# A scan's weight loading and constant building moved into the stage before it

## The chip, the cores and the metric

The kernel runs on one core of a Trainium2 chip. The metric is the device time of one execution in microseconds (us); the time given for a kernel is the median of its runs. The engines are named as in the profile: PE (TensorE, matrix products), PEld (its weight loads), DVE (VectorE), ACT (ScalarE), POOL (GpSimd) and SP (SyncE, which here only issues transfers). Each engine runs its own program in order, and semaphores tie the programs together.

## The reference, cut to what matters

Four sublayers follow one another, each with a residual and a layer norm: a scan, a mixture of experts, an attention and a second mixture of experts. The change lies in the first. Its reference:

```python
x_sub = x[:, ::2]                                      # 2048 of 4096 tokens, 256 features
x_sub = x_sub * rsqrt(mean(square(x_sub), -1) + EPS) * g_norm
xz = einsum('bld,ed->ble', x_sub, w_in) + b_in         # 512 wide
x_proj, gate = split(xz, 2, axis=-1)
c_sum = Cm.sum(axis=0)                                 # Cm is [256, 64]
def step(h, xt):                                       # h is [B, 256, 64]
    h = tanh(h * A + xt[:, :, None] * Bm)
    y = h @ c_sum + Dv * xt
    return h, y
h_last, ys = scan(step, h0, swapaxes(x_proj, 0, 1))
out = swapaxes(ys, 0, 1) * silu(gate)
out = repeat(einsum('bld,ed->ble', out, w_out) + b_out, 2, axis=1)
```

## The kernel before

The scan sublayer runs in stages: `project_in`, `load_scan_weights`, `scan_chunks`, and then `project_out`. Each stage is a block in which every engine has a program of its own. At the end of a block all engines meet, so that nothing of the next stage starts before the slowest engine of the last one has come.

`project_in` works on the 2048 tokens in four chunks of 512 (NC = 4, CH = 512); the 256 features lie on 128 partitions in DH = 2 halves. SP issues the loads of the tokens (L86), of `g_norm`, `b_in` and `w_in` (L89 to L93), and eight stores of zeros, 1 MB each, into the DRAM tensor `inbox` (L97), which a later stage needs. DVE squares the tokens (L121), PE sums the squares over the features with a matrix of ones, into PSUM bank c for chunk c (L144), ACT takes the root (L170), DVE the reciprocal (L125), and DVE scales the tokens (L128, two halves each). PE then makes four products for each chunk (L159): e = 0 and 1 are x_proj, which ACT copies into `xpT` (L176, semaphore `drained`), and e = 2 and 3 are the gate, of which ACT takes the sigmoid (L181) and DVE makes silu (L135, semaphore `gated`). PE may write a bank again only when it is drained or gated. In DVE's program all eight instructions of L135 come after all four chunks of L125 and L128. POOL has nothing in this stage but five memsets and the identity matrix (L102 to L108).

`load_scan_weights` has five transfers on SP: A, Bm, Cm and Dv (L194, L195) and a store of `xpT` to the DRAM tensor `x_proj` (L197, semaphore `x_saved`). When the four loads have landed, DVE copies A into PSUM (L209) and PE sums Cm over the features with the ones matrix into bank 1 (L203); DVE copies that sum twice into `csum` (L211, L212).

`scan_chunks` cuts the sequence into eight chunks that are scanned side by side, each with a warm-up of WARM = 20 steps: (20 + 256) = 276 steps in all, in blocks of BL = 12. In every step, in three groups, DVE multiplies the state by A (L280) and adds x times B (L285), and ACT takes tanh (L360). POOL makes the products x times B ahead of DVE (L334), with room for RING_X = 4 steps; its x comes from a slab that ACT copies (L349). PE makes the outputs of a block of 12 steps after that block is done, with 64 diagonal matrices, one for each state, as its weights (L379). DVE builds these ahead of its first step: it clears the first state (L262) and then writes 64 matrices of 128x128, each the identity times one column of `csum` (L264). They lie in the tile `stream`, which is free until the scan is over. `x_saved` is waited for by DVE before it overwrites `xpT`, after the third block.

## Time and profile before

| | |
|---|---|
| median of 3 runs | 3964.82 us (3960.57 to 3975.85) |
| the profiled execution's own time | 3958.41 us |
| its span, first to last instruction | 3956.8 us |
| mean granted clock of PE, as a share of full speed | 0.906 |
| `project_in` (to the end of the last L135) | 0 to 53.89 us |
| `load_scan_weights` (to the end of L212) | 53.89 to 59.39 us |
| `scan_chunks` before its first step (first L280) | 59.39 to 79.64 us |
| the scan's steps, to the last output | 79.64 to 808.9 us |

A row of the time line gives the start in us, the length in us, engine, line, operation, the tile written and the tiles read, shapes, the number of instructions merged into the row, and in square brackets how long the engine was idle before and what ended that. Merged rows are as long as from the first start to the last end.

### The profile page before, as it was taken

The page shows a single profiled execution, that of the slowest core. Times are in us where ns is not written, and L with a number is a line of the kernel's source. Part 1 is how long each engine was busy: PE and PEld are TensorE (multiplying, and loading weights), DVE is VectorE, ACT ScalarE, POOL GpSimd, SP SyncE. Part 2 cuts the span into 40 slices and gives each one's busy share as a digit, 9 for nine tenths or more (in the row PEclk, how much of TensorE's full clock was granted, in tenths as well). Part 3 has the DMA queues.
Part 4 walks back from the last instruction along what each step waited for, and adds up shares of the span by engine and source line. Part 5 has one row for each costly group of instructions (what it writes and reads, how often), then busy time and mean ns, then how long its engine had stood idle before and what let it go on. Part 6 is the DMA issues. An engine that isn't in the chain of part 4 may idle for free. (4 is left out here: it accounts for less than half of the span.)

```text
span 3956.8 us, 70342 instructions
## 1 busy us (share of the span) xinstructions
PE 3296.1 (83%) x25130; PEld 2356.1 (60%) x25130; DVE 2956.1 (75%) x5189; ACT 1989.2 (50%) x4068; POOL 1121.4 (28%) x1381
## 2 busy tenths in 40 slices
PE   4477776780799956799999999999999955999997
PEld 1477776740688855544555555555555424888886
DVE  7999999941344446688888888888889406888888
ACT  2544444410444412256777777777777832333333
POOL 2888888705222242000111111112021030000000
PEclk7788888875899967788999999999999977999999
DMA  3000000012222135520303031221200000000001
GB/s 135 1 1 0 0 0 0 0 46 105 94 85 85 53 100 158 119 38 7 45 13 45 13 45 24 36 35 26 42 18 11 9 24 9 13 12 12 12 12 43
DMA packets 85212, 150.95 MB, mean 38 GB/s; under 512 B 16625, under 2 KB 53382, under 8 KB 83251
## 3 DMA queue, kind: packets, MB, share of 16 engines
q1 hardware_dynamic: 64626, 104.12, 10.9%
q0 software_dynamic: 19584, 42.14, 3.5%
q10 hardware_dynamic: 768, 1.57, 0.3%
q8 instruction: 146, 2.39, 0.3%
q14 instruction: 88, 0.71, 0.1%
HBM read 90.60 MB, written 57.41 MB: 37 GB/s over the span
## 5 line engine op out<-in xcount | busy, mean ns | idle before, releaser
L1724 DVE TENSOR_REDUCE row_max<-psum 128x2 f32<-128x1024 f32 (+2 forms) x1152 | 1250.4, 1131 | 219.1 <-PE psum L1598 164.2
L1677 ACT ACTIVATE probs_T<-psum 128x512 f32<-128x512 f32 (+3 forms) x2304 | 1120.8, 566 | 366.0 <-PE psum L1622 283.6
L1622 PE MATMUL psum<-q_rows,k_rows 50*128 50x512 f32 (+3 forms) x2304 | 771.6, 440 | 15.1 <-ACT probs_T L1677 11.5
L379 PE MATMUL psum<-h_hist,stream 128*128 128x192 f32 x2816 | 502.8, 344 | 246.4 <-ACT h_hist L360 246.4
L1598 PE MATMUL psum<-k_rows,q_rows 48*128 48x512 f32 (+3 forms) x2304 | 641.1, 451 | 39.3 <-DVE row_max L1724 23.8
L334 POOL TENSOR_TENSOR x_times_b<-x_slab,B_sb 128x384 f32<-128x384 f32 (+1 forms) x828 | 625.4, 818 | 149.3 <-DVE psum L285 91.1
L379 PEld LDWEIGHTS psum<-h_hist,stream 128*128 128x128 f32 x2816 | 496.4, 203 | 252.7 <-ACT h_hist L360 154.6
L1642 PE MATMUL psum<-probs_T,v_all 128*17 128x256 f32 (+1 forms) x8704 | 600.3, 378 | 1.0 <-issue 1.0
L1622 PEld LDWEIGHTS psum<-q_rows,k_rows 50*128 50x128 f32 x2304 | 364.7, 187 | 328.5 <-ACT probs_T L1677 278.3
L360 ACT ACTIVATE h_hist<-psum 128x384 f32<-128x384 f32 (+1 forms) x828 | 339.4, 453 | 378.4 <-DVE psum L285 378.4
L1972 PE MATMUL psum<-x_T,w_part 128*128 128x512 f32 x1632 | 404.3, 397 | 24.8 <-POOL w_part L2032 24.8
L1598 PEld LDWEIGHTS psum<-k_rows,q_rows 48*128 48x128 f32 x2304 | 286.9, 191 | 151.7 <-DVE row_max L1724 96.3
L285 DVE TENSOR_TENSOR psum<-psum,x_times_b 128x384 f32<-128x384 f32 (+1 forms) x828 | 372.9, 508 | 0.0
L280 DVE TENSOR_TENSOR psum<-h_hist,psum 128x384 f32<-128x384 f32 (+1 forms) x828 | 371.2, 506 | 0.5 <-ACT h_hist L360 0.2
L1642 PEld LDWEIGHTS psum<-probs_T,v_all 128*17 128x17 f32 x8704 | 210.5, 97 | 259.4 <-ACT probs_T L1677 80.9
L1972 PEld LDWEIGHTS psum<-x_T,w_part 128*128 128x128 f32 x1632 | 301.0, 190 | 85.5 <-POOL w_part L2032 24.9
L1567 POOL DMA_DIRECT2D o_raw<-o_acc x64 | 37.0, 578 | 1092.1 <-ACT o_acc L1689 1057.6
L2071 DVE SCALAR_TENSOR_TENSOR stream<-psum,comb,stream 128x256 f32<-128x256 f32 x544 | 236.4, 476 | 0.6 <-PE psum L1984 0.6
L1984 PEld LDWEIGHTS psum<-w_part,hidden_T 128*128 128x128 f32 x1632 | 214.4, 192 | 28.6 <-DVE hidden_T L2057 15.6
L1984 PE MATMUL psum<-w_part,hidden_T 128*128 128x256 f32 x1632 | 219.4, 285 | 14.2 <-DVE hidden_T L2057 14.2
L832 PE MATMUL psum<-xeT_part,w_part 128*128 128x512 f32 x768 | 183.2, 398 | 25.4 <-ACT hT_part L873 12.8
L2032 POOL TENSOR_TENSOR w_part<-attn_T,w_part 128x768 fp32r<-128x768 f32 x17 | 31.5, 1853 | 599.1 <-ACT w_part L1996 493.7
(212 smaller groups left out, 3260.2 us busy)
## 6 DMA issues: line engine op xcount, KB each, us to landing
w_raw<-in_w SPq DMA_DIRECT2D x16, 1024.0 KB, 8.4
qk_rows<-qk_split SPq DMA_DIRECT2D x64, 256.0 KB, 3.0
q_rows<-qk_rows SPq DMA_DIRECT2D x42, 256.0 KB, 12.0
k_rows<-qk_rows SPq DMA_DIRECT2D x42, 256.0 KB, 16.8
inbox<-zeros SPq DMA_DIRECT2D x8, 1024.0 KB, 10.5
xe_sb<-inbox SPq DMA_DIRECT2D x8, 1024.0 KB, 6.0
outbox<-ye_sb POOLq DMA_DIRECT2D x8, 1024.0 KB, 10.4
o_raw<-o_acc POOLq DMA_DIRECT2D x64, 128.0 KB, 2.1
```

The costliest lines, as they stand in the source:

```text
L280: dve.tensor_tensor(part(ha, i), part(prev, i), over_chunks(A, i), ALU.mult).then_inc(ha_ready, 1)
L285: dve.tensor_tensor(u(i), part(ha, i), part(xb[:, t % RING_X], i), ALU.add).then_inc(u_ready, 1)
L334: pool.tensor_tensor(out, x, b, ALU.mult).then_inc(xb_ready, 1)
L360: act.activation(part(hist[:, slot, t], i), u(i), ACT.Tanh).then_inc(h_ready, 1)
L379: last = pe.matmul(ps[:, 1 + j, 0:BL * DH * CHUNKS], diag[:, s, :], hist[:, j, :, :, :].rearrange("p t h (s c) -> p (t h) s c", s=NS)[:, : ...
L1598: last = pe.matmul(ps[:, bank_of_S(s, j), 0:width], q[at, b, i * P:(i + 1) * P], kk[at, b, mm * CH:mm * CH + width], start=True, stop=not ...
L1622: last = pe.matmul(ps[:, bank, o:CH], kk[at, b, kt * P:(kt + 1) * P], q[at, b, qc * CH + o:(qc + 1) * CH], start=True, stop=not diag)
L1642: last = pe.matmul(ps[at:at + HD + 1, 7, lo:HALF], k.v[:, kt, 2 * (n // 4) + j, :], pt[:, u % RING_P, j, HALF * half + lo:HALF * (half + 1 ...
L1677: act.activation(pt[:, u % RING_P, j, o:CH], ps[:, S_BANKS + at_item % RING_ST, o:CH], ACT.Exp, scale=SCALE).then_inc(taken, 1)
L1724: dve.tensor_reduce(mx[:, n % 4, heads[0]:heads[-1] + 1, QT * c + i % QT, mm], ps[:, banks, 0:width], AX.X, ALU.max).then_inc(maxed, 1)
L1972: last = pe.matmul(ps[:, 2 * half + c % 2, :], w_part[:, b, wp, at:at + INTER], xT[:, xp, h, c * CH:(c + 1) * CH], start=(n == 0 and h == ...
L1984: last = pe.matmul(ps[:, 4 + 2 * (c % 2) + s // 2, (s % 2) * D:(s % 2 + 1) * D], hT[:, c % 2, hp, s * P:(s + 1) * P], w_part[:, b, wp, WCO ...
```

## The change

Nothing of the computation changes. The stage `load_scan_weights` is gone. Its four loads stand in `project_in` on SP, behind the token loads and ahead of the `inbox` stores; the store of `x_proj` stands behind these, after a wait for all eight drained halves. PE sums Cm between its first and its second chunk of products, after a wait for the four loads and for ACT's last root (bank 1 holds chunk 1's sums until then). DVE copies the sum and A between its last scaling and its first gate. POOL builds the diagonal matrices, 16 at a time, four instructions, when the first copy of the sum is there; PE's wait for them in the scan is now for `k.diags` at 4.

```diff
@@ project_in
+        cm = sb("cm_sb", [P, DH, NS])
+        diag = k.stream[:, :, :].rearrange("p n c -> p (n c)").rearrange("p (s q) -> p s q", s=NS)
...
         @block.sync
...
+            for dst, src in ((k.A, a["A"]), (k.B, a["Bm"]), (cm, a["Cm"])):
+                sp.dma_start(dst[:, :, :], src.rearrange("(h p) s -> p h s", p=P)).then_inc(ab_in, 16)
+            sp.dma_start(k.Dv[:, :], a["Dv"].rearrange("(h p) -> p h", p=P), allow_slow_non_contiguous=True).then_inc(ab_in, 16)
             sp.wait_ge(k.zeros_ready, 1)
...
+            sp.wait_ge(drained, DH * NC)
+            sp.dma_start(a["x_proj"].rearrange("(h p) t -> p h t", p=P), k.xpT[:, :, WARM:WARM + TP]).then_inc(k.x_saved, 16)
+            sp.wait_ge(ab_in, 64)
...
         @block.gpsimd
...
+            pool.wait_ge(const_ready, 5)
+            pool.wait_ge(copied, 1)
+            for s in range(0, NS, 16):
+                pool.tensor_tensor(diag[:, s:s + 16, :], k.ident[:, :].unsqueeze(1).to_broadcast([P, 16, P]),
+                                   k.csum[:, 0, s:s + 16].unsqueeze(2).to_broadcast([P, 16, P]), ALU.mult).then_inc(k.diags, 1)
...
         @block.vector
...
+                if c == NC - 1:
+                    dve.wait_ge(csum, 1)
+                    dve.tensor_copy(k.csum[:, 0, :], ps[:, 1, 0:NS]).then_inc(copied, 1)
+                    dve.tensor_copy(k.csum[:, 1, :], ps[:, 1, 0:NS]).then_inc(copied, 1)
+                    dve.tensor_copy(ps[:, 0, 0:DH * NS].rearrange("p (h s) -> p h s", h=DH), k.A[:, :, :]).then_inc(a_copied, 1)
...
         @block.tensor
...
+                if c == 1:
+                    pe.wait_ge(ab_in, 64)
+                    pe.wait_ge(root, NC)
+                    for h in range(DH):
+                        last = pe.matmul(ps[:, 1, 0:NS], k.ones[:, :], cm[:, h, :], start=(h == 0), stop=(h == DH - 1))
+                    last.then_inc(csum, 1)
...
-def load_scan_weights(nc, k, a):
...
@@ scan_chunks
-            for s in range(NS):
-                last = dve.tensor_scalar(diag[:, s, :], k.ident[:, :], k.csum[:, 0, s:s + 1], None, ALU.mult)
-            last.then_inc(diags, 1)
...
-            pe.wait_ge(diags, 1)
+            pe.wait_ge(k.diags, 4)
...
@@ build_scan
-        load_scan_weights(nc, k, a)
```

DVE's program from its last scaling in `project_in` to its first steps in the scan, before (a row is a line of the kernel, the operation, the tiles and the shape; branches end a stage's program):

```order
L128 SCALAR_TENSOR_TENSOR xsT<-xsT,g_norm_sb,rms 128x512 x2
L135 SCALAR_TENSOR_TENSOR gateT<-psum,b_in_sb,gate_sig 128x512 x8
L64 UNCONDITIONAL_BRANCH
L206 UNCONDITIONAL_BRANCH
L209 COPY psum<-A_sb 128x128
L211 COPY csum_sb<-psum 128x64
L212 COPY csum_sb<-psum 128x64
L186 UNCONDITIONAL_BRANCH
L260 UNCONDITIONAL_BRANCH
L262 MEMSET h_hist 128x1024
L264 TENSOR_SCALAR stream<-ident,csum_sb 128x128 x64
L280 TENSOR_TENSOR psum<-h_hist,psum 128x384 x2
```

The same stretch of DVE's program now:

```order
L142 SCALAR_TENSOR_TENSOR xsT<-xsT,g_norm_sb,rms 128x512 x2
L146 COPY csum_sb<-psum 128x64
L147 COPY csum_sb<-psum 128x64
L148 COPY psum<-A_sb 128x128
L154 SCALAR_TENSOR_TENSOR gateT<-psum,b_in_sb,gate_sig 128x512 x8
L64 UNCONDITIONAL_BRANCH
L254 UNCONDITIONAL_BRANCH
L256 MEMSET h_hist 128x1024
L271 TENSOR_TENSOR psum<-h_hist,psum 128x384 x2
```

The three copies moved from between the stages to ahead of the gates, and the 64 instructions that build the matrices left DVE.

POOL's program from the end of its constants to its first products of the scan, before:

```order
L106 MEMSET zeros 128x256
L108 ISA
L108 AFFINE_SELECT ident<-ident 128x128
L64 UNCONDITIONAL_BRANCH
L320 UNCONDITIONAL_BRANCH
L334 ISA
L334 TENSOR_TENSOR x_times_b<-x_slab,B_sb 128x8x48 x2
L334 TENSOR_TENSOR x_times_b<-x_slab,B_sb 128x2x8x16
```

The same stretch of POOL's program now:

```order
L115 MEMSET zeros 128x256
L117 ISA
L117 AFFINE_SELECT ident<-ident 128x128
L122 TENSOR_TENSOR stream<-ident,csum_sb 128x2048 x4
L64 UNCONDITIONAL_BRANCH
L311 UNCONDITIONAL_BRANCH
L325 TENSOR_TENSOR x_times_b<-x_slab,B_sb 128x8x48 x2
L325 TENSOR_TENSOR x_times_b<-x_slab,B_sb 128x2x8x16
```

Four instructions of 2048 elements on each partition stand now between the identity matrix and the end of POOL's stage.

SP's program, all of it up to the end of the scan's set-up, before:

```order
L86 DMA xsT<-in_xs_T 128x2x512 x3
L97 DMA inbox<-zeros 128x8x256 x8
L64 UNCONDITIONAL_BRANCH
L191 UNCONDITIONAL_BRANCH
L194 DMA A_sb<-in_A 128x2x64
L194 DMA B_sb<-in_Bm 128x2x64
L194 DMA cm_sb<-in_Cm 128x2x64
L195 DMA Dv_sb<-in_Dv 128x2x1
L197 DMA x_proj<-xpT 128x2x2048
```

The same stretch of SP's program now:

```order
L89 DMA xsT<-in_xs_T 128x2x512 x3
L99 DMA A_sb<-in_A 128x2x64
L99 DMA B_sb<-in_Bm 128x2x64
L99 DMA cm_sb<-in_Cm 128x2x64
L100 DMA Dv_sb<-in_Dv 128x2x1
L103 DMA inbox<-zeros 128x8x256 x8
L106 DMA x_proj<-xpT 128x2x2048
```

The four loads moved ahead of the eight stores of zeros, and the store of `x_proj` follows these within the same stage.

## Rows read from the trace of the kernel before

**Rows 1.** Busy us of each engine (instructions), PE's clock, DMA share, by stretch:

```profile
35.00:54.00 19.00, 17.38 (x40) 7.46 (x40) 5.04 (x7) 6.87 (x10) 0.00 (x0) 1.00 0.00 0
60.00:80.00 20.00, 0.00 (x0) 0.00 (x0) 20.00 (x66) 0.05 (x1) 9.52 (x12) 0.50 0.10 44
```

**Rows 2.** Time line of DVE, 30 to 83 us:

```profile
32.81 1.41 DVE L128 SCALAR_TENSOR_TENSOR xsT<-xsT,g_norm_sb,rms 128x512 f32<-128x512 f32 x2
34.15 1.40 DVE L135 SCALAR_TENSOR_TENSOR gateT<-psum,b_in_sb,gate_sig 128x512 f32<-128x512 f32 x2
...
53.14 0.75 DVE L135 SCALAR_TENSOR_TENSOR gateT<-psum,b_in_sb,gate_sig 128x512 f32<-128x512 f32 x1 [0.97 <-ACT gate_sig L181]
57.86 0.29 DVE L209 COPY psum<-A_sb 128x128 f32<-128x128 f32 x1 [3.98 <-DMA Dv_sb<-in_Dv]
59.04 0.22 DVE L211 COPY csum_sb<-psum 128x64 f32<-128x64 f32 x1 [0.88 <-PE psum L203]
...
59.96 0.91 DVE L262 MEMSET h_hist<- 128x1024 f32 x1 [0.56 <-PEq L186]
60.79 18.93 DVE L264 TENSOR_SCALAR stream<-ident,csum_sb 128x128 f32<-128x128 f32 x64
79.64 1.34 DVE L280 TENSOR_TENSOR psum<-h_hist,psum 128x384 f32<-128x384 f32 x3
...
82.17 1.00 DVE L280 TENSOR_TENSOR psum<-h_hist,psum 128x384 f32<-128x384 f32 x2
```

**Rows 3.** Time line of PE, several stretches from 19 to 810 us:

```profile
20.24 12.23 PE L159 MATMUL psum<-xsT,w_in_sb 128*128 128x512 f32 x24 [2.76 <-DVE xsT L128]
...
34.95 17.43 PE L159 MATMUL psum<-xsT,w_in_sb 128*128 128x512 f32 x40 [2.47 <-DVE gateT L135]
57.88 1.12 PE L203 MATMUL psum<-cm_sb,ones 128*128 128x64 f32 x4 [5.50 <-DMA Dv_sb<-in_Dv]
...
141.47 23.82 PE L379 MATMUL psum<-h_hist,stream 128*128 128x192 f32 x128 [82.47 <-ACT h_hist L360]
...
785.70 22.59 PE L379 MATMUL psum<-h_hist,stream 128*128 128x192 f32 x128 [8.12 <-ACT h_hist L360]
```

**Rows 4.** Time line of ACT, 24 to 60 us:

```profile
29.08 0.69 ACT L181 ACTIVATE gate_sig<-psum,b_in_sb 128x512 f32<-128x512 f32 x1 [0.34 <-PE psum L159]
...
52.42 0.69 ACT L181 ACTIVATE gate_sig<-psum,b_in_sb 128x512 f32<-128x512 f32 x1 [1.03 <-PE psum L159]
59.69 0.36 ACT L349 ACTIVATE x_slab<-xpT 128x192 f32<-128x192 f32 x1 [6.59 <-PEq L186]
```

**Rows 5.** Time line of SP, the issues of transfers, 0 to 1000 us:

```profile
3.02 1.49 SPq L86 DMA_DIRECT2D xsT<-in_xs_T  x3
4.55 23.03 SPq L97 DMA_DIRECT2D inbox<-zeros  x8
...
56.12 0.47 SPq L197 DMA_DIRECT2D x_proj<-xpT  x1
```

**Rows 6.** Transfers, 0 to 200 us: issues, KB each, median us to landing:

```profile
inbox<-zeros SPq DMA_DIRECT2D x8, 1024.0 KB, 10.5
...
Dv_sb<-in_Dv SPq DMA_DIRECT2D x1, 1.0 KB, 2.2
```

**Rows 7.** POOL's groups by shape, whole span (busy us, mean ns, idle before):

```profile
L938 POOL TENSOR_TENSOR w_part<-w_raw,w_part 128x2048 fp32r<-128x2048 f32 x8 | 36.8, 4602 | 94.7 <-ACT w_part L859 94.7
...
L2032 POOL TENSOR_TENSOR w_part<-attn_T,w_part 128x768 fp32r<-128x768 f32 x17 | 31.5, 1853 | 599.1 <-ACT w_part L1996 493.7 <-ACT w_part L2012 105.4
```

**Rows 8.** Time line of POOL, 0 to 90 us (idle in brackets):

```profile
60.14 9.52 POOL L334 TENSOR_TENSOR x_times_b<-x_slab,B_sb 128x384 f32<-128x384 f32 x12 [58.21 <-ACT x_slab L349]
...
84.05 2.26 POOL L334 TENSOR_TENSOR x_times_b<-x_slab,B_sb 128x384 f32<-128x384 f32 x3 [0.26 <-DVE psum L285]
```

**Rows 9.** L264 alone, by stretch: busy us of DVE (instructions begun), clock, DMA:

```profile
64.00:66.00 2.00, 2.00 (x3) 0.50 0.00 0
72.00:76.00 4.00, 4.00 (x22) 0.50 0.00 0
```

More of the change, by code:

```diff
@@ L78, in project_in @@
             "inv_rms_ready", "xz_ready", "xz_drained", "gate_sigmoid", "gate_done"))
+        cm = sb("cm_sb", [P, DH, NS])
+        ab_in, csum, copied, a_copied = (sem(n) for n in ("ab_in", "csum_ready", "csum_copied", "a_copied"))
+        diag = k.stream[:, :, :].rearrange("p n c -> p (n c)").rearrange("p (s q) -> p s q", s=NS)
         NC = TP // CH
@@ L181, in _ @@
                         act.activation(sig[:, n % 2, :], ps[:, 4 + n % 2, :], ACT.Sigmoid, bias=b[:, e:e + 1]).then_inc(sigmoid, 1)
-def load_scan_weights(nc, k, a):
-    with ExitStack() as loc:
-        cm = k.sbuf(loc)("cm_sb", [P, DH, NS])
-        ab_in, csum, copied, a_copied = k.sem("ab_in"), k.sem("csum_ready"), k.sem("csum_copied"), k.sem("a_copied")
-        block = loc.enter_context(nc.Block())
-        @block.sync
-        def _(sp):
-            for dst, src in ((k.A, a["A"]), (k.B, a["Bm"]), (cm, a["Cm"])):
-                sp.dma_start(dst[:, :, :], src.rearrange("(h p) s -> p h s", p=P)).then_inc(ab_in, 16)
-            sp.dma_start(k.Dv[:, :], a["Dv"].rearrange("(h p) -> p h", p=P), allow_slow_non_contiguous=True).then_inc(ab_in, 16)
-            sp.dma_start(a["x_proj"].rearrange("(h p) t -> p h t", p=P), k.xpT[:, :, WARM:WARM + TP]).then_inc(k.x_saved, 16)
-        @block.tensor
-        def _(pe):
-            pe.wait_ge(ab_in, 64)
-            for h in range(DH):
-                last = pe.matmul(k.psum[:, 1, 0:NS], k.ones[:, :], cm[:, h, :], start=(h == 0), stop=(h == DH - 1))
-            last.then_inc(csum, 1)
-        @block.vector
-        def _(dve):
-            dve.wait_ge(ab_in, 64)
-            dve.tensor_copy(k.psum[:, 0, 0:DH * NS].rearrange("p (h s) -> p h s", h=DH), k.A[:, :, :]).then_inc(a_copied, 1)
-            dve.wait_ge(csum, 1)
-            dve.tensor_copy(k.csum[:, 0, :], k.psum[:, 1, 0:NS]).then_inc(copied, 1)
-            dve.tensor_copy(k.csum[:, 1, :], k.psum[:, 1, 0:NS]).then_inc(copied, 1)
 def scan_chunks(nc, k, a):
@@ L237, in scan_chunks @@
         count = sb("seam_count", [P, 1])
-        xs_ready, xb_ready, ha_ready, u_ready, h_ready, y_done, y_taken, h_zero, diags, warm_kept = (
-            sem("ch_" + n) for n in ("xs", "xb", "ha", "u", "h", "y_done", "y_taken", "h_zero", "diag", "warm"))
+        xs_ready, xb_ready, ha_ready, u_ready, h_ready, y_done, y_taken, h_zero, warm_kept = (
+            sem("ch_" + n) for n in ("xs", "xb", "ha", "u", "h", "y_done", "y_taken", "h_zero", "warm"))
         compared, counted, summed, told = (sem("ch_" + n) for n in ("compared", "counted", "summed", "told"))
@@ L2109, in build_program @@
         k.x_saved = k.sem("x_saved")
+        k.diags = k.sem("diags")
         k.zeros_ready, k.inbox_zeroed = k.sem("zeros_ready"), k.sem("inbox_zeroed")
```

## The prediction

> **What bounds the kernel now.** I read the page's slices first, to see that the change touches only the first stages. Then come the busy times by stretch: while the input projection runs, from 35 to 54 us, PE is busy for 17.38 of 19 us and POOL for none; from 60 to 80 us DVE is busy all the time and PE for none [rows 1]. So between the projection and the scan DVE alone sets the pace, and ahead of it POOL has nothing to do.
>
> DVE's time line gives that stretch step by step [rows 2]. The last gate ends at 53.14 + 0.75 = 53.89 us. The copy of A then waits 3.98 us for the last of the four loads, the copy of the sum for PE, and the stage ends at 59.39. The memset of the scan begins 0.57 later and takes 0.91. The 64 diagonal matrices take from 60.79 to the first step at 79.64. From the last gate to the first step 25.75 us pass, in which no step of the scan runs. All the stages are bound by meetings of the engines, so a microsecond taken out here is one off the whole, as long as what follows keeps its length.
>
> **What the diagonal matrices are needed for.** PE's first output in the scan starts at 141.47 us, 62 us after the first step, and waits for ACT's states [rows 3]. The matrices are early by far; they cost time only since they stand ahead of the steps in DVE's program.
>
> **The change part by part.**
>
> 1. The loads. A, Bm, Cm and Dv are issued behind the last token load, so from about 4.5 us on [rows 5]. Alone Dv landed 2.2 us after its issue; the slowest kind here, the stores of zeros, took 10.5 [rows 6]. A load issued by 6.5 us that takes as long as those lands at 17 us. PE asks for it after its first chunk, which ends at 29.0 us: the second gate sigmoid of that chunk waits for PE until 29.08 [rows 4]. Cost: none. The wait for the last root is over too: in ACT's program all four roots stand ahead of these sigmoids. What this removes is the wait for the loads in the old stage. The stores of zeros move back by four issues, some 2 us; SP ends their issue at 27.58 [rows 5] and has nothing then until 50 us, so nothing waits.
>
> 2. The sum of Cm on PE took 1.12 us at low clock [rows 3]. It now delays the second chunk's first two products by at most that. These end at 20.24 + 12.23 = 32.47, and PE then idles for 2.47 us until the first gate is done [rows 3]. The cover is larger than the cost; without it the cost would be 1.12 us.
>
> 3. The three copies on DVE stand now between the last scaling (end 34.22) and the first gate [rows 2]. The gate frees the bank that PE waits for, so they do cost: twice 0.22 and 0.29, 0.73 us by their lengths, and 0.29 if the shorter ones are hidden by overlap [rows 2]. I take 0.73. From that gate on the rest of the projection is one chain: PE's 17.43 us without a gap [rows 3], ACT's last sigmoid at 52.42 [rows 4], the last gate [rows 2]. So the last gate ends at 53.89 + 0.73 = 54.62.
>
> 4. The matrices on POOL. 4 x 2048 = 8192 elements on each partition. A two-input POOL instruction of 2048 elements took 4602 ns [rows 7]: 4 x 4.602 = 18.4 us. The nearest rows on either side: 2.26 us for the 1024 elements of one step, with broadcast operands as here, gives 18.1 [rows 8]; 1853 ns for 768 gives 19.8, and the first twelve products, 9.52 us for 4096, give 19.0 [rows 7, 8]. POOL can start when the first copy of the sum is there, 34.22 + 0.22 = 34.44, so it ends at 52.9 (52.5 to 54.2). That is ahead of the last gate at 54.62: hidden, by 1.7 us at my value and 0.4 at the slow end. Every microsecond beyond would be paid in full at the meeting.
>
> 5. Into the scan. One stage and one meeting are gone. From the end of a stage's last DVE instruction to the memset 0.57 us, then 0.91, and the first step may start: 54.62 + 1.48 = 56.1 us, against 79.64. POOL's head start in x times B is gone too: before it had 12 products ready, now it starts just ahead of DVE. ACT's slab starts 0.30 after the stage's end and takes 0.36 [rows 4], POOL 0.09 later, at 55.4; it makes a step's products in 2.26 us [rows 8], so by 57.6. DVE's adds of the first step begin when its three multiplications are through, at 56.1 + 1.34 = 57.4 [rows 2]. The first add needs only the first product, by 56.2 (9.52/12 = 0.79 us each) [rows 8], and the third product is there by 57.6, when DVE has still two adds ahead of it. A step of DVE takes 2.53 us (79.64 to 82.17) [rows 2], and POOL, faster by 0.26, draws ahead. Cost: none.
>
> 6. The store of `x_proj` is issued when the last half is drained, some 6 us ahead of 56.12 [rows 5]. It is needed after the third block, 36 steps on. No cost.
>
> 7. The scan's end. After the last step DVE waits for PE's last block of outputs, 22.59 us in this execution; the first block took 23.82 [rows 3]. Which of the two falls to the last block depends on how PE's clock stands at that moment, and a shifted start may change it: 0 to 1.2 us, taken as 0, since the scan's own pattern is unchanged.
>
> Sum: 79.64 - 56.1 = **23.5 us saved**. By the bounds: 24.0 with overlapped copies; 19.5 if, against every row, POOL ended 4 us after the gates. Against the profiled execution's own time: 3958.41 - 23.5 = 3934.9. That execution lies 6.4 us under the median of the runs shown, so for the median I say 3964.82 - 23.5 = 3941.3, rounded to **3941**.
>
> **A rule weighed against the rows.** Beside POOL's first products DVE began 3 of its matrices in 2 us, alone 22 in 4 us [rows 9]: 0.67 against 0.18 us each. The two engines do block one another here. The Trainium skill, SBUF — State Buffer, section Who interferes with whom, says that they share one pair of ports as an exclusive lock, that `tensor_scalar` can take it, and that a DVE instruction with at most one SBUF input outside the two-port modes does not contend. By that rule the gates (one input from PSUM, one from SBUF) would not be held up by POOL. The scan's adds, with the same kinds of input, keep their step of 2.53 us beside POOL [rows 2, 8], so the trace agrees.
>
> The rows above put POOL's instruction at 4602 ns; for the same matrices DVE took 18.9 us [rows 2]. The Trainium skill, GPSIMD Engine Reference, section When to use GPSIMD, advises against elementwise work there, as about twice as slow as DVE. Taken against DVE's 18.9 us that would be 38 us of POOL. The rows don't bear it out for this case, since DVE's time was 64 short instructions, half of them beside POOL; but it is a rival.
>
> **The rivals.**
>
> A. POOL's build is late. What speaks for it is the small margin, 1.7 us, and a shape that no row shows (2048 elements, both operands broadcast). Each us beyond 54.62 counts. At twice DVE's 18.93, 37.9 us, POOL ends at 72.3 and 17.7 of the 23.5 are given back: 3959. At 3 ns an element, 24.6 us, it ends at 59.0: 3946. All four POOL rows lie between 2.2 and 2.4 ns an element. Chance 0.08.
>
> B. The four loads are caught among the 8 MB of zeros. The zeros are issued until 27.58, by then 2 us later, and take 10.5 more [rows 5, 6]: 40 us at the worst. PE's second chunk would start 11 us late, of which its 2.5 us of idle time cover some: about 8 us lost, 3949. Against it: they are issued ahead of all the zeros. Chance 0.05.
>
> C. The scan's pace falls, the slower side. Without its head start, POOL must keep DVE's pace from the first step. The point from which it decides is a product time of 2.53 us a step; from 2.53 + 23.5/276 = 2.62 us on the kernel is slower than before. At 2.70 us a step it loses 0.17 x 276 = 47 us and gains 23.5: 3988. For it: the beginning ran at 9.52/4 = 2.38 a step, not 2.26. Against it: in all the later steps POOL waits 0.26 us for DVE, so the pace is shown over the whole scan [rows 8]. Chance 0.03.
>
> D. The change doesn't bring what it says: the start of the scan moves forward, but the time is lost again behind it (PE's clock in the last outputs, or the stages after). Then the time stays between 3950 and 3965. Nothing in the rows names more than 1.2 us. Chance 0.04.
>
> **How the numbers follow.** The forecast has 0.80, A 0.08, B 0.05, C 0.03, D 0.04. About 0.5%, or 19.8 us, is what a measurement can tell from no change here, so faster begins at 3945.0. The three runs before spread over 15 us, and a median of runs may well be 4 us off; 3941 lies 4 under the bound. I give the forecast 0.85 to be told as faster: 0.68, and 0.02 from the milder half of A. The rest of the forecast (0.12), most of A, B and D are within 0.5%: 0.27. C is slower, 0.03. The range for 8 in 10: downwards the profiled execution's own basis, 3935, less 3 us; upwards the spread of the runs, A at 3 ns and B, 3951.
>
> **What would show it.** The first multiplication of a step at 56 us (55.5 to 58), the last gate at 54.6, POOL's four instructions at 4.5 to 4.8 us each with the last end ahead of that gate, PE without a wait for the loads between its first two chunks, steps of 2.52 us from the first on, and the last output 23 to 24 us earlier than before. A POOL end behind the last gate means A; a wait of PE at 29 us for Dv means B; DVE waiting for x times B means C. The prediction is wrong if the first step starts after 60 us, or if the first step starts in time and the end doesn't follow.

## The result

| | before | changed |
|---|---|---|
| median | 3966.13 us, 5 runs (3960.57 to 3977.30) | 3938.36 us, 5 runs (3930.04 to 3942.48) |
| ratio, 95% interval | | 0.993 (0.9911 to 0.9949) |
| profiled execution's own time; span | 3958.41; 3956.8 us | 3930.04; 3928.6 us |
| last gate ends | 53.89 us | 53.32 us |
| first step of the scan | 79.64 us | 54.83 us |
| last output of the scan | 808.86 us | 784.00 us |

The kernel is faster by 20 to 35 us, 28 by the medians. The profile puts the gain where it was looked for: the first step starts 24.81 us earlier, and the last output is 24.86 us earlier.

The changed kernel's time line of DVE, from the first reciprocal to the second step, answers to [rows 2]:

```profile
14.28 3.35 DVE L139 RECIPROCAL rms<-rms 128x512 f32<-128x512 f32 x1
...
31.79 1.41 DVE L142 SCALAR_TENSOR_TENSOR xsT<-xsT,g_norm_sb,rms 128x512 f32<-128x512 f32 x2
33.12 0.22 DVE L146 COPY csum_sb<-psum 128x64 f32<-128x64 f32 x1
33.26 0.22 DVE L147 COPY csum_sb<-psum 128x64 f32<-128x64 f32 x1
33.39 0.29 DVE L148 COPY psum<-A_sb 128x128 f32<-128x128 f32 x1
33.58 1.40 DVE L154 SCALAR_TENSOR_TENSOR gateT<-psum,b_in_sb,gate_sig 128x512 f32<-128x512 f32 x2
...
45.70 0.75 DVE L154 SCALAR_TENSOR_TENSOR gateT<-psum,b_in_sb,gate_sig 128x512 f32<-128x512 f32 x1 [0.97 <-ACT gate_sig L206]
...
52.57 0.75 DVE L154 SCALAR_TENSOR_TENSOR gateT<-psum,b_in_sb,gate_sig 128x512 f32<-128x512 f32 x1 [0.97 <-ACT gate_sig L206]
53.88 0.91 DVE L256 MEMSET h_hist<- 128x1024 f32 x1 [0.56 <-PEq L64]
54.83 1.36 DVE L271 TENSOR_TENSOR psum<-h_hist,psum 128x384 f32<-128x384 f32 x3
56.10 1.35 DVE L276 TENSOR_TENSOR psum<-psum,x_times_b 128x384 f32<-128x384 f32 x3
57.36 1.35 DVE L271 TENSOR_TENSOR psum<-h_hist,psum 128x384 f32<-128x384 f32 x3
```

Between the last gate and the first step there is only the stage's end (0.56 us) and the memset; the wait for the loads, the sum and the 64 matrices are gone from this line. The copies overlap: the first gate starts 1.79 us after the last scaling, against 1.34 before [rows 2], so they cost 0.45 us. The steps run at 2.53 us from the first on.

POOL in the same kernel, the build and the first products of the scan, which answer to [rows 8]:

```profile
33.49 14.31 POOL L122 TENSOR_TENSOR stream<-ident,csum_sb 128x2048 f32<-128x2048 f32 x4 [31.57 <-DVE csum_sb L147]
54.05 29.54 POOL L325 TENSOR_TENSOR x_times_b<-x_slab,B_sb 128x384 f32<-128x384 f32 x40 [6.25 <-ACT x_slab L340]
```

The build ends at 47.80, 5.5 us ahead of the last gate. PE, which answers to [rows 3]:

```profile
19.21 8.80 PE L184 MATMUL psum<-xsT,w_in_sb 128*128 128x512 f32 x16 [2.76 <-DVE xsT L142]
27.85 0.56 PE L171 MATMUL psum<-cm_sb,ones 128*128 128x64 f32 x4
28.24 3.65 PE L184 MATMUL psum<-xsT,w_in_sb 128*128 128x512 f32 x8
34.38 17.43 PE L184 MATMUL psum<-xsT,w_in_sb 128*128 128x512 f32 x40 [2.48 <-DVE gateT L154]
```

There is no wait for the loads ahead of the sum of Cm, and the sum takes half of what it took before; PE's idle time before the gate is as long as it was. The transfers, which answer to [rows 6] (KB each, median us to landing):

```profile
A_sb<-in_A SPq DMA_DIRECT2D x1, 64.0 KB, 7.4
...
Dv_sb<-in_Dv SPq DMA_DIRECT2D x1, 1.0 KB, 6.2
```

Among the token loads the four take 6.1 to 7.4 us instead of 1.8 to 2.2, and are there some 14 us before PE asks.

**A measure without the scatter of the start.** The first reciprocal starts at 14.28 us here and at 15.30 in the kernel before, whose row is this:

```profile
15.30 3.34 DVE L125 RECIPROCAL rms<-rms 128x512 f32<-128x512 f32 x1
```

Nothing of the change lies ahead of it but the order of transfers, and it scatters (next section). From there to the first step it is 79.64 - 15.30 = 64.34 us before and 54.83 - 14.28 = 40.55 us now: 23.8 us less. The experiments are compared by this time from the first reciprocal to the first step, called the distance below.

### The profile page after: what moved, and what is told of

It reads as the page before. It is cut to its first block and busy times, and to the rows that moved or that the text cites. A ratio compares the mean times of both kernels' runs of the same rounds, so it can differ in the third digit from the quotient of the medians.

```text
span 3928.6 us, 70266 instructions
## 1 busy us (share of the span) xinstructions
PE 3287.0 (84%) x25130; PEld 2351.6 (60%) x25130; DVE 2937.5 (75%) x5125; ACT 1988.5 (51%) x4068; POOL 1134.7 (29%) x1385
## 5 line engine op out<-in xcount | busy, mean ns | idle before, releaser
L276 DVE TENSOR_TENSOR psum<-psum,x_times_b 128x384 f32<-128x384 f32 (+1 forms) x828 | 390.6, 573 | 0.0
L271 DVE TENSOR_TENSOR psum<-h_hist,psum 128x384 f32<-128x384 f32 (+1 forms) x828 | 389.1, 571 | 0.4 <-ACT h_hist L351 0.2
L1975 PE MATMUL psum<-w_part,hidden_T 128*128 128x256 f32 x1632 | 219.5, 285 | 14.3 <-DVE hidden_T L2048 14.3
```

The lines of the kernel that those rows point to most:

```text
L271: dve.tensor_tensor(part(ha, i), part(prev, i), over_chunks(A, i), ALU.mult).then_inc(ha_ready, 1)
L276: dve.tensor_tensor(u(i), part(ha, i), part(xb[:, t % RING_X], i), ALU.add).then_inc(u_ready, 1)
L1975: last = pe.matmul(ps[:, 4 + 2 * (c % 2) + s // 2, (s % 2) * D:(s % 2 + 1) * D], hT[:, c % 2, hp, s * P:(s + 1) * P], w_part[:, b, wp, WCO ...
```

## The experiments

| kernel | first reciprocal | first step | distance | against before | ratio to before, 95% interval |
|---|---|---|---|---|---|
| before | 15.30 | 79.64 | 64.34 | | |
| changed | 14.28 | 54.83 | 40.55 | -23.8 | 0.9911 to 0.9949 |
| changed again (e9) | 15.11 | 55.66 | 40.55 | -23.8 | 0.9911 to 0.9949 |
| matrices on DVE (e1) | 15.37 | 74.67 | 59.30 | -5.0 | 0.9978 to 1.0013 |
| built twice (e2) | 15.01 | 64.45 | 49.44 | -14.9 | 0.9931 to 0.9977 |
| loads behind zeros (e3) | 16.85 | 64.01 | 47.16 | -17.2 | 0.9939 to 0.9974 |
| zeros in scan (e4) | 14.36 | 56.61 | 42.25 | -22.1 | 0.9913 to 0.9963 |
| gates earlier (e8) | 14.74 | 52.55 | 37.81 | -26.5 | 0.9893 to 0.9929 |
| gates earlier, zeros in scan (e7) | 14.77 | 51.16 | 36.39 | -28.0 | 0.9897 to 0.9941 |
| POOL in the old stage (e5) | 16.96 | 76.78 | 59.82 | -4.5 | 0.9966 to 0.9994 |

Times are in us, from one profile of each kernel; a thousandth of the ratio is 4 us. In all but e8 the change of the distance lies inside the interval of the whole kernel's time: as far as intervals 11 to 20 us wide can tell, what is gained ahead of the first step arrives at the end. The profiles say it more finely: from the first step to the last output the scan takes 729.1 to 730.4 us in all ten.

**The changed kernel again (e9).** No edit.

> The changed kernel itself once more, so that the next two have a neighbour on the same chip, and to see what scatters between two of its profiles. Expected: 0.993 of the kernel before. The second token chunk's squares have started between 9.8 and 10.9 us in three kernels with the same order of transfers; if that is scatter, the first step starts between 54.8 and 56.0 us here, and the distance from the last gate's end to the first step stays 1.5 us.

Measured: 3938.95 us, 0.993. The distance is the same to a hundredth, while the first reciprocal comes 0.83 us later. So of the 24.8 us of the first profile 23.8 are the change's by the distance, and the 1.0 ahead of it is no more than scatter: with the changed order of transfers the first reciprocal starts between 14.28 and 16.65 us in seven profiles (e6 and e10, below, among them), with the order of before at 15.30 and 16.96 (e5). A small effect of the order is not excluded. The second token chunk's squares, at 9.64, came a little earlier than the range said; what was late here were the sums of squares (6.37 us on PE instead of 5.42).

**The matrices back on DVE (e1).**

```diff
-            for s in range(0, NS, 16):
-                pool.tensor_tensor(diag[:, s:s + 16, :], k.ident[:, :].unsqueeze(1).to_broadcast([P, 16, P]),
-                                   k.csum[:, 0, s:s + 16].unsqueeze(2).to_broadcast([P, 16, P]), ALU.mult).then_inc(k.diags, 1)
...
             dve.memset(hist[:, 1, BL - 1, :, :], 0.0).then_inc(h_zero, 1)
+            for s in range(NS):
+                last = dve.tensor_scalar(diag[:, s, :], k.ident[:, :], k.csum[:, 0, s:s + 1], None, ALU.mult)
+            last.then_inc(k.diags, 1)
...
-            pe.wait_ge(k.diags, 4)
+            pe.wait_ge(k.diags, 1)
```

> The changed kernel with one part undone: DVE builds the 64 matrices in the scan again, POOL builds none; the stage between stays gone and the loads stay early. Theory (time between the last gate and the first step is on the path, POOL hides the build): the first step starts 18.9 us later than in the changed kernel (54.83 + 18.9 = 73.7 us), the last output moves by the same, and the kernel takes 3938 + 19 = 3957 us, so that only about 6 us of the gain are left. Rival (what is saved at the start is lost again behind the scan, or most of the gain comes from elsewhere): less than 12 us slower than the changed kernel.

Measured: 3963.65 us. DVE's time line:

```profile
55.81 18.94 DVE L253 TENSOR_SCALAR stream<-ident,csum_sb 128x128 f32<-128x128 f32 x64
74.67 1.34 DVE L269 TENSOR_TENSOR psum<-h_hist,psum 128x384 f32<-128x384 f32 x3
```

The distance is 18.75 us longer than in the changed kernel, as expected; the first step itself came 1.0 us later than the 73.7, since the first reciprocal did. The time came out 7 us above the 3957; the interval of the ratio, -9 to +5 us against before, still holds the 5.0 us that the early loads and the dropped stage should leave, and can't tell them from nothing. The rival (less than 12 us slower) is out: it is 25 us slower by the medians.

**Built twice (e2).** The four POOL instructions run twice.

```diff
-            for s in range(0, NS, 16):
...
+            for turn in range(2):
+                for s in range(0, NS, 16):
+                    pool.tensor_tensor(diag[:, s:s + 16, :], k.ident[:, :].unsqueeze(1).to_broadcast([P, 16, P]),
+                                       k.csum[:, 0, s:s + 16].unsqueeze(2).to_broadcast([P, 16, P]), ALU.mult).then_inc(k.diags, 1)
+                if turn == 0:
+                    pool.wait_ge(k.diags, 4)
...
-            pe.wait_ge(k.diags, 4)
+            pe.wait_ge(k.diags, 8)
```

> POOL builds the matrices twice, eight instructions instead of four, the second four behind the first. Theory (the build costs nothing up to the last gate at 53.32 us, and each microsecond beyond it in full, at the meeting of the engines): POOL runs from 33.5 for 2 x 14.3 = 28.6 us to 62.1, the stage ends there, the first step starts 1.5 us later at 63.6, 8.8 us later than in the changed kernel, 3947 us. Rival (POOL's work is not waited for until PE needs the matrices at 117 us): no change, 3938.

Measured: 3946.88 us. POOL's line and DVE's:

```profile
34.23 28.68 POOL L123 TENSOR_TENSOR stream<-ident,csum_sb 128x2048 f32<-128x2048 f32 x8 [32.30 <-DVE csum_sb L150]
```

```profile
53.31 0.75 DVE L157 SCALAR_TENSOR_TENSOR gateT<-psum,b_in_sb,gate_sig 128x512 f32<-128x512 f32 x1 [0.97 <-ACT gate_sig L209]
63.51 0.91 DVE L259 MEMSET h_hist<- 128x1024 f32 x1 [9.45 <-PEq L64]
64.45 1.36 DVE L274 TENSOR_TENSOR psum<-h_hist,psum 128x384 f32<-128x384 f32 x3
```

POOL ends at 62.91; DVE, done at 54.06, waits 9.45 us for it at the stage's end. The distance grows by 8.89 us, against 8.8 expected. The cover ends at the last gate, and beyond it every microsecond is paid, although PE's first output follows only some 60 us later.

**POOL in the old stage (e5).** The kernel before, with the build on POOL in `load_scan_weights`.

```diff
+        @block.gpsimd
+        def _(pool):
+            pool.wait_ge(copied, 1)
+            for s in range(0, NS, 16):
+                pool.tensor_tensor(diag[:, s:s + 16, :], k.ident[:, :].unsqueeze(1).to_broadcast([P, 16, P]),
+                                   k.csum[:, 0, s:s + 16].unsqueeze(2).to_broadcast([P, 16, P]), ALU.mult).then_inc(k.diags, 1)
...
-            for s in range(NS):
-                last = dve.tensor_scalar(diag[:, s, :], k.ident[:, :], k.csum[:, 0, s:s + 1], None, ALU.mult)
-            last.then_inc(diags, 1)
...
-            pe.wait_ge(diags, 1)
+            pe.wait_ge(k.diags, 4)
```

> The kernel before with one part of the change alone: the stage between projection and scan and its late loads stay, but POOL builds the matrices within that stage, where nothing covers it. Theory (POOL needs 14.3 us for what takes DVE 18.9, and the rest of the gain is cover): the build runs from 59.4 to 73.7 us, the first step starts 1.5 us later at 75.2 us, 4.4 us earlier than in the kernel before, 3958 to 3960 us. Rival (POOL is faster only in the projection, since DVE does little there): it takes 18.4 us as the trace of the kernel before had it for that many elements, and the first step starts at 79.3 us.

Measured: 3959.20 us. DVE's line:

```profile
60.77 0.21 DVE L220 COPY csum_sb<-psum 128x64 f32<-128x64 f32 x1
75.84 0.91 DVE L270 MEMSET h_hist<- 128x1024 f32 x1 [14.85 <-PEq L186]
76.78 1.36 DVE L285 TENSOR_TENSOR psum<-h_hist,psum 128x384 f32<-128x384 f32 x3
```

The distance is 4.5 us shorter than before (expected 4.4), and POOL's four instructions take 14.30 us here, as beside the projection. So of the 23.8 us some 4.5 come from building on POOL with nothing to hide it, 5.0 from the early loads and the dropped stage together (e1); the other 14.3, by difference, agree with the build's own 14.31, hidden. The 4.5 don't show that POOL is the quicker engine for this work: in the kernel before DVE began 14 of its 64 instructions in the 9 us beside POOL's first products, and the rest in the 10 us after them. At the 22 in 4 us of [rows 9], 64 would take DVE alone 11.6 us. That is an estimate; no run had DVE build the matrices with POOL silent.

**The loads behind the zeros (e3).**

```diff
-            for dst, src in ((k.A, a["A"]), (k.B, a["Bm"]), (cm, a["Cm"])):
-                sp.dma_start(dst[:, :, :], src.rearrange("(h p) s -> p h s", p=P)).then_inc(ab_in, 16)
-            sp.dma_start(k.Dv[:, :], a["Dv"].rearrange("(h p) -> p h", p=P), allow_slow_non_contiguous=True).then_inc(ab_in, 16)
             sp.wait_ge(k.zeros_ready, 1)
             for e in range(8):
                 sp.dma_start(a["inbox"][e * 1024:(e + 1) * 1024, :].rearrange("(s p) c -> p s c", p=P),
                              k.zeros[:, :].unsqueeze(1).to_broadcast([P, 8, D])).then_inc(k.inbox_zeroed, 16)
+            for dst, src in ((k.A, a["A"]), (k.B, a["Bm"]), (cm, a["Cm"])):
+                sp.dma_start(dst[:, :, :], src.rearrange("(h p) s -> p h s", p=P)).then_inc(ab_in, 16)
+            sp.dma_start(k.Dv[:, :], a["Dv"].rearrange("(h p) -> p h", p=P), allow_slow_non_contiguous=True).then_inc(ab_in, 16)
```

> The four loads are issued behind the eight stores of zeros instead of ahead of them; all else as in the changed kernel. Theory (transfers of one queue land in about the order of issue, and the stores of zeros also slow the token loads): the loads are issued from 27.6 us and land at 33 to 38 us, PE waits for them between its first two chunks, and its last 20.6 us of products run from there, so that the last gate ends near 60 us, 6 to 7 us later than in the changed kernel (3945 us). The second token chunk's squares start at about 10.7 us as in the kernel before, not at 9.8. Rival for the loads (they pass the stores): PE waits for less than 3 us and the time is 3938 to 3940. Rival for the tokens (the 1.0 us was scatter): squares at 9.8 us here too.

Measured: 3942.98 us. PE's line:

```profile
36.53 1.12 PE L171 MATMUL psum<-cm_sb,ones 128*128 128x64 f32 x4 [5.93 <-DMA Dv_sb<-in_Dv]
37.44 23.56 PE L184 MATMUL psum<-xsT,w_in_sb 128*128 128x512 f32 x48
```

PE waits 5.93 us for the loads and then runs its last products partly at the lower clock: the granted clock is 0.50 from 36 to 40 us, and the 48 products take 23.56 us, where 48 without a gap take 20.82 at full clock (e8, below). The distance grows by 6.6 us. This is the event of rival B with its price: here the order of issue on SP decides, and the change has it right. On the tokens the run is no evidence: the squares of the second chunk started at 10.54 here, but at 10.86 in e1 and 10.50 in e2 too, where the loads stand ahead of the zeros. Scatter alone covers that 1.0 us.

**The zeros in the scan (e4).** The eight stores of zeros are issued by SP in `scan_chunks`.

```diff
@@ project_in
-            sp.wait_ge(k.zeros_ready, 1)
-            for e in range(8):
-                sp.dma_start(a["inbox"][e * 1024:(e + 1) * 1024, :].rearrange("(s p) c -> p s c", p=P),
-                             k.zeros[:, :].unsqueeze(1).to_broadcast([P, 8, D])).then_inc(k.inbox_zeroed, 16)
@@ scan_chunks
+        @block.sync
+        def _(sp):
+            sp.wait_ge(k.zeros_ready, 1)
+            for e in range(8):
+                sp.dma_start(a["inbox"][e * 1024:(e + 1) * 1024, :].rearrange("(s p) c -> p s c", p=P),
+                             k.zeros[:, :].unsqueeze(1).to_broadcast([P, 8, D])).then_inc(k.inbox_zeroed, 16)
```

> The eight stores of zeros are issued by SP in the scan's stage, where no other transfer runs, instead of in the projection. Theory (the stores of zeros compete with the token loads): the second token chunk lands as early as in the changed kernel or up to 1 us earlier, so the first step moves forward by 0 to 1 us (53.8 to 54.8), and nothing is lost in the scan, since its steps wait for no transfer: 3937 to 3938 us. Rival (the zeros cost the scan something there, or are late for the scatter that follows): the last output comes later than 784 us.

Measured: 3941.24 us, and a first step 1.70 us later by the distance, where the theory had it up to 1 us earlier. The tokens were not late (first reciprocal at 14.36). PE's line:

```profile
19.30 7.10 PE L180 MATMUL psum<-xsT,w_in_sb 128*128 128x512 f32 x16 [2.76 <-DVE xsT L138]
...
34.46 19.13 PE L180 MATMUL psum<-xsT,w_in_sb 128*128 128x512 f32 x40 [4.18 <-DVE gateT L150]
```

The first chunk took 7.10 us, where it had taken 8.80 in the changed kernel; PE then idled for 4.18 instead of 2.48 us, and the last 40 products took 19.13 instead of 17.43: 1.70 us won, idled away and lost again. The clock says the same. By stretch (busy us of PE, PEld, DVE, ACT and POOL with counts, then granted clock, DMA share, GB/s), the zeros in the scan:

```profile
20.00:34.00 14.00, 10.29 (x27) 4.44 (x25) 13.89 (x13) 5.77 (x8) 0.42 (x1) 1.00 0.00 0
34.00:54.00 20.00, 19.13 (x40) 8.11 (x40) 4.82 (x7) 6.55 (x10) 13.89 (x4) 0.91 0.11 46
```

and the changed kernel:

```profile
20.00:34.00 14.00, 11.90 (x27) 5.01 (x25) 13.89 (x13) 5.87 (x8) 0.51 (x1) 0.88 1.06 357
34.00:54.00 20.00, 17.43 (x40) 7.54 (x40) 5.60 (x9) 7.23 (x11) 13.80 (x4) 1.00 0.24 98
```

In e4 the clock is full while PE works on the first chunk, and falls behind the longer idle time (0.50 from 36 to 38 us). The rival is out: the last output comes at 785.67 us, but the scan from its first step on takes 729.1 us, as in the changed kernel, so only the start was later.

Why the clock is full in the first chunk without the zeros stays open, but it is not PE's work ahead of it. In e7 and e8 below, which differ by the zeros alone, PE's sums of squares start at 11.51 us in both and take 5.44 and 5.42, and PE then idles for 2.76 in both; yet from 20 to 24 us e7, without the zeros, and e8, with them, read:

```profile
20.00:24.00 4.00, 4.00 (x10) 1.71 (x9) 3.96 (x3) 0.35 (x1) 0.00 (x0) 1.00 0.00 0
```

```profile
20.00:24.00 4.00, 4.00 (x6) 1.52 (x5) 3.96 (x3) 0.32 (x1) 0.00 (x0) 0.57 1.06 363
```

All ten profiles with 340 to 390 GB/s of transfers there show the fall to the lower level in the first chunk, and neither of the two without. That the transfers bring it about is likely by this, and not shown.

**The first gates ahead of the last scaling (e8).** `gates(c)` holds the two instructions of L154 for chunk `c`, unchanged.

```diff
             for c in range(NC):
+                if c == NC - 1:
+                    gates(0)
                 cols = slice(c * CH, (c + 1) * CH)
                 dve.wait_ge(root, c + 1)
...
-            for c in range(NC):
+            for c in range(1, NC):
+                gates(c)
```

> The changed kernel, with DVE's first two gates ahead of its last reciprocal and scaling instead of behind them and the three copies. Theory (PE's idle time of 2.48 us in the second chunk is a wait for that gate, and the copies cost 0.46 us only since they stand ahead of it): PE runs its last three chunks without a gap, so the last gate ends 2.5 + 0.5 = 3.0 us earlier as seen from the start of PE's first products, the first step likewise. POOL's 14.3 us, from the copies on, still end ahead of the last gate. Rival (the gate in the middle holds up the last scaling, and PE then waits for that): PE idles ahead of its fourth chunk, and the first step moves by less than 1 us.

Measured: 3932.50 us. PE's line:

```profile
28.71 20.82 PE L189 MATMUL psum<-xsT,w_in_sb 128*128 128x512 f32 x48
```

One row instead of two: no gap. 3.65 + 2.48 + 17.43 = 23.56 us have become 20.82, 2.74 less, and the distance is 2.74 shorter. The 3.0 expected counted the copies twice; they were part of the idle time of 2.48. The whole kernel gained against before 28 to 42 us, and the start explains 26.5; the 1.6 us at least on top are not explained, and one 95% interval of nine that misses is no finding. That e8 is faster than the changed kernel is shown for the start; for the whole their intervals overlap.

**Both (e7).** The edits of e4 and e8 together.

> The same with the eight stores of zeros issued in the scan's stage. With the stores moved but the gates as they were, PE's first chunk took 7.10 instead of 8.80 us, but PE then idled for 4.18 us and its last 40 products took 19.13 instead of 17.43 us, so that the first step came at 56.61 instead of 54.83 us. Theory (what was gained in the first chunk was lost to the longer idle time and the lower clock after it): without the idle time both stay, the first step starts at 50 to 51 us, and POOL's build, from 35 to 49 us, is then what the stage's end waits for or nearly so. Rival (the clock falls for another reason): the last chunks run at the low clock again for some of their length, and the first step is not ahead of that of the kernel that keeps the zeros.

Measured: 3935.74 us. PE, POOL and DVE:

```profile
19.71 7.10 PE L185 MATMUL psum<-xsT,w_in_sb 128*128 128x512 f32 x16 [2.76 <-DVE xsT L148]
...
27.04 20.82 PE L185 MATMUL psum<-xsT,w_in_sb 128*128 128x512 f32 x48
```

```profile
35.31 14.31 POOL L118 TENSOR_TENSOR stream<-ident,csum_sb 128x2048 f32<-128x2048 f32 x4 [33.37 <-DVE csum_sb L153]
```

```profile
48.62 0.75 DVE L128 SCALAR_TENSOR_TENSOR gateT<-psum,b_in_sb,gate_sig 128x512 f32<-128x512 f32 x1 [0.97 <-ACT gate_sig L207]
50.21 0.91 DVE L264 MEMSET h_hist<- 128x1024 f32 x1 [0.84 <-PEq L64]
```

As the theory had it, but for the first step at 51.16 instead of 50 to 51: the short first chunk stays, the last 48 products run at full clock, and now POOL, done at 49.62, is later than the last gate at 49.37: DVE's wait at the stage's end is 0.84 us instead of 0.56. The distance is 4.2 us below the changed kernel's, the shortest of all, with the cover used up. The whole kernel's time, 0.9919 of before, can't be told from that of e8 or of the changed kernel.

**What makes POOL's build quick (e6, e10).** The changed kernel with eight more POOL instructions of 2048 elements behind the last gate, DVE idle, each form as a product and as a difference. `full`, `half` and `gate` are 2048 elements of the tiles `xpT` (two halves) and `gateT`, `rows` is the identity and `cols` the sum of Cm, broadcast as in the build.

```diff
@@ e6
+            for x, y in ((full, full), (rows, full), (full, cols), (rows, cols)):
+                for op in (ALU.mult, ALU.subtract):
+                    pool.tensor_tensor(probe[:, :, :], x, y, op).then_inc(probed, 1)
...
@@ e10
+            for x, y in ((full, gate), (full, half), (rows, rows), (full, rows)):
```

> The changed kernel with eight more POOL instructions of 2048 elements behind the last gate, one after another, into a tile that nothing reads, while DVE is idle: both operands full rows; the first broadcast over the 16 matrices; the second one value for 128 elements; both broadcast as in the build. Each once as a product and once as a difference. The question: the build took 3.58 us an instruction, a difference of 2048 elements in the kernel before 4.60. Theory 1 (the operand that stays the same for 128 elements makes it cheap): 3.6 us in the third and fourth form, 4.6 in the first two. Theory 2 (a product is cheaper than a difference): 3.6 us for all products, 4.6 for all differences. Theory 3 (the 4.60 us came from work of the other engines or from the rounded output type): about 3.6 us for all eight. The kernel as a whole takes some 35 us longer than the changed one, by design.

Measured, e6 (ns shortest, median and longest; first and last start):

```profile
L134 POOL TENSOR_TENSOR probe_sb<-xpT x2: 3598/3598/3598, 55.6 to 59.2; 128x2048 f32<-128x2048 f32 x2
L134 POOL TENSOR_TENSOR probe_sb<-ident,xpT x2: 4492/4492/4493, 62.9 to 67.5; 128x2048 f32<-128x2048 f32 x2
L134 POOL TENSOR_TENSOR probe_sb<-xpT,csum_sb x2: 3606/3606/3607, 72.1 to 75.7; 128x2048 f32<-128x2048 f32 x2
L134 POOL TENSOR_TENSOR probe_sb<-ident,csum_sb x2: 3606/3606/3606, 79.4 to 83.1; 128x2048 f32<-128x2048 f32 x2
```

None of the three theories: product and difference take the same, and the first form, a tile with itself, is as quick as those with the one-value operand. That led to the second probe.

> The same probe with four other forms, each once as a product and once as a difference, behind the last gate while DVE is idle. In the first probe a tile with itself took 3.60 us, the identity's rows with another tile 4.49, and anything with the one-value operand 3.61. Open: whether 4.49 is the price of two operands from different places, as in the row of the kernel before at 4.60, or that of a broadcast row. Forms here: two full tiles; two places of one tile; the identity's rows with themselves; a full tile with the identity's rows. Theory 1 (two places cost 4.5): 4.5, 4.5, 3.6, 4.5 us. Theory 2 (broadcast rows beside full rows cost it): 3.6, 3.6, 3.6, 4.5 us.

Measured, e10:

```profile
L135 POOL TENSOR_TENSOR probe_sb<-xpT,gateT x2: 4492/4492/4492, 55.8 to 60.4; 128x2048 f32<-128x2048 f32 x2
L135 POOL TENSOR_TENSOR probe_sb<-xpT x2: 4493/4494/4494, 65.0 to 69.6; 128x2048 f32<-128x2048 f32 x2
L135 POOL TENSOR_TENSOR probe_sb<-ident x2: 3598/3598/3598, 74.1 to 77.8; 128x2048 f32<-128x2048 f32 x2
L135 POOL TENSOR_TENSOR probe_sb<-xpT,ident x2: 4492/4492/4493, 81.5 to 86.0; 128x2048 f32<-128x2048 f32 x2
```

Theory 1 in all four forms: two operands that advance through different places cost 4.49 us; the same place twice, or one value held for 128 elements, 3.60. In the kernel before the row of two places reads 4.60 [rows 7]; these 0.11 us are left, and the runs don't say whether they come from the rounded output type or from the other engines. The Trainium skill, GPSIMD Engine Reference, section Performance versus the Vector engine, gives 4497 ns for a `tensor_tensor` addition of 2048 elements and puts it down to two operands taking turns at one read port. The 4492 ns agree with it; that the price falls where both operands can come from one place or one stands still is in line with it, and only these runs show it.

## Why the prediction was right, step by step

The mechanism, the sum and the sign held: 23.5 us forecast, 23.8 by the distance, 24.8 in the profile with 1.0 of scatter, 20 to 35 for the whole kernel. 3938.36 us lies 2.6 under the 3941 and inside the range. Some of the named signs missed. The last gate at 53.32 us, the first step at 54.83 and the last output, 24.86 us earlier, lie outside what was named by the scatter of the start and the shorter copies; POOL's instructions took 3.6 us each instead of 4.5 to 4.8. Point by point:

1. *The loads.* No wait, as forecast. They took 6.1 to 7.4 us rather than 2.2, inside the 10.5 that the bound allowed. The issue of the zeros began 3.5 us later, but did not end later as I had it: at 27.61 us against 27.58 [rows 5].
2. *The sum on PE.* 0.56 us, half of the 1.12 of the row at the lower clock [rows 3]; hidden either way.
3. *The copies.* 0.45 us against 0.73. I took their full lengths although L212 showed an overlap: it starts at 59.18 us, when L211 still runs to 59.26. The three overlap each other and the scaling. These 0.28 us are all but the whole difference between 23.5 and 23.8.
4. *The build on POOL.* 14.31 us against 18.4, below the lower bound of 18.1: the term that was mis-sized. The row of 4602 ns [rows 7] had two operands from different places, the build has one that stands still, and e6 and e10 show that this is most of the difference (0.89 of 1.02 us). It did no harm since the term is hidden; the margin at the last gate was 5.5 us, not 1.7. The products of the scan, which I called broadcast as here, were no match either, and I scaled them with all that a short instruction costs. By shape they took 898 ns for 384 elements and 660 for 256 in the kernel before: read as a straight line 1.86 ns an element and 0.18 us for each instruction, which would have put the build at some 16 us instead of 18.1 (an estimate).
5. *Into the scan.* 1.51 us from the last gate's end to the first step (forecast 1.48). No add waits for POOL: the second step's multiplications start 2.53 us after those of the first.
6. *The store of `x_proj`* is issued at 49.13 us instead of 56.12 [rows 5]; nothing waits for it.
7. *The scan's end.* First step to last output is 729.2 us before and in the changed kernel's first profile, but that the term is 0 is in part luck: in its second profile (e9) the last block of outputs takes 23.85 us instead of 22.88, and the scan 730.3. Of the 0 to 1.2 us that I allowed, either end could have come.

```profile
760.54 22.88 PE L370 MATMUL psum<-h_hist,stream 128*128 128x192 f32 x128 [7.82 <-ACT h_hist L351]
```

```profile
761.53 23.85 PE L370 MATMUL psum<-h_hist,stream 128*128 128x192 f32 x128 [6.86 <-ACT h_hist L351]
```

On the rule about ports: the gates took 0.75 us each beside POOL's build (the one at 45.70), as without it [rows 2]. The Trainium skill, SBUF — State Buffer, section Who interferes with whom, would have it so for a single input from SBUF; the trace agrees.

In weighing the other rule I wrote that half of DVE's 64 instructions ran beside POOL. It was half of their time, but only 14 of them (see e5).

The rivals: A did not come, and e2 shows what it would have cost, microsecond for microsecond beyond the last gate. B has its price in e3, 6.6 us against my 8, and did not come since the loads stand first. C did not come. D is out for the scan; behind it the stages scatter. The attention's second product runs from 1660.2 to 3208.3 us in the kernel before and from 1628.6 to 3177.8 in the changed one, 1548 and 1549 us, but over 1560.8 us in the changed kernel's second profile and 1578.7 in e4, here before and e4:

```profile
L1642 PE MATMUL psum<-probs_T,v_all x8704: 272/379/634, 1660.2 to 3208.3; 128*17 128x256 f32 x182, 128*17 128x128 f32 x16
```

```profile
L1636 PE MATMUL psum<-probs_T,v_all x8704: 272/379/634, 1631.3 to 3210.0; 128*17 128x256 f32 x182, 128*17 128x128 f32 x16
```

None of the kernels differs there. That is why the spans of single executions can't rank these kernels. Whether the 2 to 4 us by which the median fell further than the first step moved are more than scatter stays open: 42 runs of the kernel before have a mean of 3964.8 and 11 of the changed one 3938.4, 26.4 apart, with standard deviations of 7.1 and 5.6. The standard error of that difference is about 2.0, so at 95% it lies between 22 and 30, and 23.8 is inside.

## What to carry to other kernels

In this kernel work that a later stage needs, and that sat between two stages on an engine of the path, cost its full length there (e1); on an engine that is idle in the stage before it cost nothing until that stage's last instruction, and its full overrun from there on (e2). So compare its end with that instruction, not with the moment at which its result is needed. When a start-up scatters, measure from a point behind the scatter (here the first reciprocal): the two profiles of the changed kernel then agreed to 0.01 us, where its whole runs spread over 19.

## What the runs showed of the hardware

A two-operand POOL instruction of 2048 elements on each partition took 4.49 us when its operands advanced through two different places, and 3.60 us when they were the same place or one of them held a value for 128 elements; product and difference cost the same (e6, e10). And a faster first chunk on PE bought nothing while PE then had to wait: in e4 the 1.70 us gained came back as 1.70 us more of idle time, and the clock, 1.00 in the stretch before, was 0.91 in the next, which cost another 1.70; with the idle time taken out (e7) the gain stayed. What gave the faster chunk was moving 8 MB of stores out of that stage, the only difference between the changed kernel and e4 and between e8 and e7: the granted clock in that chunk was 1.00 in both kernels without the stores, and fell to 0.50 for a time in all ten with them. How the stores do it is open.
